# Moving the third set of transpositions and the projection behind half of the value products in a two-layer gated attention kernel

## The reference

```python
x = x + jnp.tanh(g_xattn[1]) * _L1_xattn_ref(_layernorm(x), ctx_1024, Wq, bq, Wk, bk, Wv, bv, Wo, bo)
# 16 heads of 8 features
q = (query_states @ Wq.T + bq)   # k and v likewise, from the context
scores = jnp.einsum('bhqd,bhkd->bhqk', q * SCALE, k)
attn = jax.nn.softmax(scores, axis=-1)
ctx = jnp.einsum('bhqk,bhkd->bhqd', attn, v)
out = ctx @ Wo.T + bo
```

## Time and profile before

| what | us |
|---|---|
| median of 3 runs | 304.81 (303.15 to 305.63) |
| the profiled execution, its own time | 303.55 |
| its span in the trace | 301.7 |
| PE busy | 277.1 (92%) |
| DVE busy | 236.2 (78%) |
| ACT busy | 130.8 (43%) |
| POOL busy | 85.5 (28%) |

### The profile page before, as it was taken

How to read it: one execution, slowest core, us unless ns; L and a number is a source line. 1 busy time by engine, 2 the same in 40 slices (tenths; PEclk the granted TensorE clock), 3 DMA queues, 4 the chain that set the end, 5 groups by cost and what they waited for, 6 DMA issues and landing times.

```text
span 301.7 us, 5454 instructions
## 1 busy us (share of the span) xinstructions
PE 277.1 (92%) x1646; PEld 208.5 (69%) x1646; DVE 236.2 (78%) x661; ACT 130.8 (43%) x275; POOL 85.5 (28%) x161
## 2 busy tenths in 40 slices
PE   6799899999989979869899899899999999999993
PEld 5588577667566557458788788798966676676661
DVE  4887889859988987887888888887578779776572
ACT  1497552342242242385565565565432332423320
POOL 7467010100480304322843943842100100000000
PEclk9999899999999999999999999999999999999999
DMA  6910059173262152000000000000242331521640
GB/s 212 352 53 1 4 172 245 54 235 106 55 187 76 61 174 75 0 2 0 2 1 2 2 0 3 0 2 1 80 133 70 118 131 35 185 95 33 209 147 35
DMA packets 15066, 25.26 MB, mean 84 GB/s; under 512 B 2341, under 2 KB 4339, under 8 KB 14835
## 3 DMA queue, kind: packets, MB, share of 16 engines
q1 hardware_dynamic: 12968, 23.88, 24.5%
q10 hardware_dynamic: 2072, 1.07, 1.3%
HBM read 22.98 MB, written 1.25 MB: 80 GB/s over the span
## 4 chain that ended last, share of the span: by engine, by line
PE 70%; DVE 8%; DMA 6%; ACT 5%; POOL 4%; issue 4%; SPq 0%; POOLq 0%; DVEq 0%; ACTq 0%
PE S L543 25%; PE Ybank L565 15%; PE Ybank L714 10%; DMA CR<-comb_rows 4%; PE bank L700 4%; PE S L690 3%; ACT pt L977 2%; DMA comb_rows<-ct 2%; PE Tb L483 2%; POOL KT L355 1%; PE bank L581 1%; DVE xn L1060 1%; PE Tb L728 1%; POOL xn L405 1%; DVE cmx L1337 1%
## 5 line engine op out<-in xcount | busy, mean ns | idle before, releaser
L862 ACT ACTIVATE sg<-S 128x512 f32<-128x512 f32 x64 | 38.0, 596 | 70.5 <-PE S L543 65.6
L1206 DVE TENSOR_TENSOR hb<-sg,CR 128x512 f32<-128x512 f32 x64 | 45.1, 705 | 13.9 <-DMA CR<-comb_rows 5.1
L1199 DVE TENSOR_TENSOR sg<-sg,S 128x512 f32<-128x512 f32 x64 | 43.5, 680 | 3.5 <-PE S L543 2.1
L338 POOL TENSOR_TENSOR rstd<-ve,mhalf 128x4 f32<-128x4 f32 x11 | 11.1, 1011 | 107.1 <-DVE ve L1053 107.1
L714 PE MATMUL Ybank<-VX,pt 128*128 128x128 f32 (+1 forms) x320 | 39.8, 275 | 0.0
L714 PEld LDWEIGHTS Ybank<-VX,pt 128*128 128x128 f32 (+1 forms) x320 | 37.9, 192 | 0.4
L543 PE MATMUL S<-xh,WBH 128*128 128x512 f32 x64 | 33.8, 529 | 3.1 <-DVE sg L1199 3.0
L543 PE MATMUL S<-xh,UPH 128*128 128x512 f32 x64 | 36.1, 564 | 0.0
L565 PE MATMUL Ybank<-hb,downw 128*128 128x512 f32 x64 | 33.0, 599 | 0.7 <-DVE hb L1206 0.7
L565 PE MATMUL Ybank<-hb,W2T 128*128 128x512 f32 x64 | 32.9, 597 | 0.0
L1337 DVE TENSOR_REDUCE cmx<-S 128x8 f32<-128x616 f32 x32 | 25.4, 794 | 4.6 <-PE S L690 4.3
(11 more groups left out here) (164 smaller groups left out, 500.6 us busy)
## 6 DMA issues: line engine op xcount, KB each, us to landing
CR<-comb_rows SPq DMA_DIRECT2D x64, 128.0 KB, 3.1
CR<-comb_rows SPq DMA_DIRECT2D x32, 256.0 KB, 3.3
w13raw<-in_w SPq DMA_DIRECT2D x1, 1088.0 KB, 10.9
X<-in_x SPq DMA_DIRECT2D x4, 256.0 KB, 6.3
upraw<-in_up SPq DMA_DIRECT2D x4, 256.0 KB, 4.3
out_x<-X SPq DMA_DIRECT2D x4, 256.0 KB, 3.3
cT<-in_ctxT SPq DMA_DIRECT2D x2, 308.0 KB, 5.6
CN<-in_ctx SPq DMA_DIRECT2D x1, 616.0 KB
```

What stands on the lines that cost most here:

```text
L862: A(sg[:, k % 2, :], Gb[k % 2][:], ACT.Silu).then_inc(m.s_done, 1)
L1199: V.tensor_tensor(sg[:, k % 2, :], sg[:, k % 2, :], Ub[k % 2][:], ALU.mult).then_inc(m.t2, 1)
L1206: V.tensor_tensor(hb[:, k % 2, :], sg[:, k % 2, :], CR[:, k % RING, :], ALU.mult).then_inc(m.h_done, 1)
```

## The change

In TensorE's pass, the first half of `c_mix` (block n-1) moves ahead of `c_project` and the third set of transpositions moves behind `c_project`. The new order is scores, first set, turn, second set, first half of the value products, projection, third set, wait for `c_fin` where there is one, `norm_T` or `c_query`, second half. In ScalarE's pass the copy of the third set moves behind the first half of the exponentials of block n+1. In VectorE's pass the maxima of the second half move ahead of the final addition. No instruction is added or removed.

```diff
--- before.py
+++ after.py
@@ -743,11 +743,11 @@
                     if n >= 2:
                         c_turn(*divmod(n - 2, GB))
                     c_transpose(g, t, 1)
-                    c_transpose(g, t, 2)
+                    if n:
+                        c_mix(*divmod(n - 1, GB), n == 1, 0)
                     if n >= 2:
                         c_project(*divmod(n - 2, GB))
-                    if n:
-                        c_mix(*divmod(n - 1, GB), n == 1, 0)
+                    c_transpose(g, t, 2)
                     if n >= 2 and (t < 2 or last and t == GB - 1):
                         pe.wait_ge(c_fin, START + n - 1)
                     if t == 0:
@@ -991,9 +991,9 @@
                     if t == GB - 1 and last:
                         m_route_tanh(mD, 0)
                     c_copy(g, t, 1, n == 0)
-                    c_copy(g, t, 2, n == 0)
                     if n + 1 < NB:
                         c_exps(*divmod(n + 1, GB), 0)
+                    c_copy(g, t, 2, n == 0)
                     if t == 0:
                         norm_hi(2 * NG + 2 + g, xh[:, slot(g + 1):slot(g + 1) + GT])
                     if t == 1 and not last:
@@ -1381,10 +1381,11 @@
                         route_top(mD, 0)
                         route_pick(mD, 0)
                         route_weights(mD, 0)
+                    if ahead:
+                        c_max(*divmod(n + 1, GB), 1)
                     if n >= 2:
                         c_final(*divmod(n - 2, GB))
                     if ahead:
-                        c_max(*divmod(n + 1, GB), 1)
                         c_center(*divmod(n + 1, GB), 1)
                     if t == 0:
                         norm_lo(2 * NG + 2 + g, g + 1)
```

## The result

| | before | changed |
|---|---|---|
| median of 16 runs each, us | 303.58 | 302.16 |
| ratio, 95% interval | | 0.9934 (0.9915 to 0.9954) |
| profiled execution, us | 303.55 | 302.13 |
| first score product of block 0's pass to first gate product of mixture D, us | 85.04 | 83.11 |

What follows compares the result with a forecast made beforehand. TensorE was taken to set the pace, busy 20.3 of 22.0 us. The terms 1.68 + 0.42 - 0.21 + 0.21 - 0.26 = 1.84 us, taken from 304.81, gave 303.0 us; range 301.0 to 304.8.

Steps and rivals of the forecast that it cites:

- The stall's price: TensorE's third set waits for ScalarE's copy of the first set in 11 blocks; 0.42 us per stalled block.
- The bracket's 0.23: The wait for the copy shown in block 6's TensorE rows, 0.23 us, taken as the stall's lower bound.
- VectorE just keeps up at t = 2: Blocks 2, 6, 10, 14: VectorE's subtraction allows the next scores at 4.58 against TensorE's 4.59; gain 0.42 us each.
- rival of a late VectorE: Addition or subtraction 0.4 us late at t = 2, so blocks 2, 6, 10 gain nothing; 304.2 us, chance 15%.
- The wait that takes the stall's place: Blocks at t = 0 and 1: TensorE waits for the final addition until 3.71 us; only 0.21 us gained in all.
- rival of the full gain: The wait for the final addition is hidden, so all 11 stalled blocks gain; 4.4 us, 300.4 us, chance 10%.
- t = 3: Blocks 3, 7, 11 end on the chain variances, power, keys and get 0.07 us longer each, -0.21 us.
- Last pass: Block 15 never stalled but waits for the final addition ahead of the routing transpose; it loses 0.26 us.
- ScalarE: Exponentials ahead of the third copy end by 4.0 us, before the next copy at 4.3; the reordering is hidden.
- The slower rival: The final addition, behind late second maxima in seven blocks, costs more than the stall; 3.8 us slower, 308.6, chance 5%.
- The time: Whole kernel: median 304.81 us less the summed gain of 1.84 us gives 303.0 us, 0.6% faster.

Runs made afterwards that it cites:

- e1: Changed kernel with VectorE's old order, the final addition ahead of the second maxima again; ratio 1.0028 to the kernel before, stage 86.52 us.
- e5: Changed kernel with the projection inside the first half of the value products and the final addition ahead of the second maxima at t = 0 and 1; 0.9812 of before.
- e4: Changed kernel with TensorE's new order only in blocks 1, 2, 6, 10 and 14; ratio 0.9921 to the kernel before, stage 82.96 us.
- e3: Changed kernel with TensorE's old order, keeping VectorE's and ScalarE's new ones; ratio 0.9971 to the kernel before, stage 84.32 us.
- e2: Changed kernel with ScalarE's old order, the third set's copy ahead of the exponentials' first half again; ratio 0.9918 to the kernel before.
- e8: Changed kernel with GpSimd's keys of block 4g+5 expanded at t = 2, behind the power and ahead of the normalisation; ratio 0.9869 to the kernel before.
- e6: Changed kernel with GpSimd's keys of block 4g+5 expanded at t = 2, ahead of the power and the normalisation; ratio 0.9997 to the kernel before.
- e7: Changed kernel with the edits of e5 and e6 together; ratio 0.9767 to the kernel before, stage 77.60 us.
- e9: Changed kernel with the edits of e5 and e8 together; ratio 0.9764 to the kernel before, stage 77.62 us.

## Why the forecast held, point by point

**The stall's price.** Right. 0.42 us by the spacing of starts, and blocks 2, 6, 10 and 14 lost 0.43. The bracket's 0.23 would have given about half. Block 1 was mis-sized: I took 0.42 there too, and it lost 0.57. Its rows in the kernel before:

```profile
134.55 0.60 PE L700 MATMUL Ybank<-CB,PX 128*104 128x128 f32 x4
135.50 0.41 PE L700 MATMUL bank<-CB,PX 128*128 128x128 f32 x2 [0.34 <-ACT pt L977]
```

The third set follows the second after 0.95 us, 0.51 more than the unstalled 0.44. No turn stands between the first and the second set there, so TensorE came to the wait 0.11 us sooner; block 1's own spacing would have given most of the difference.

**VectorE just keeps up at t = 2.** Right, and shown by undoing it (e1). The margin was 0.08 us before, and the swap of maxima and addition is a condition of the change, not an ornament: without it the stage is longer than before. The rival of a late VectorE falls for the changed kernel, and is exactly what e1 is. In e5 the subtraction of block 6 ends 0.44 us ahead of the next scores and the block still takes 4.58, so in the changed kernel's 4.57 it is TensorE's own work that sets the length.

**The wait that takes the stall's place.** Right in place and size. Forecast: `norm_T` and the query at 3.71; measured 3.70 and 3.69. e4 shows that these passes are worth 0.1 us at most, e5 that nothing else held them back by that much. The rival of the full gain falls for this change. In the changed kernel's trace the second half stands behind the waiting instruction in all seven places (in block 8 at 175.61, `norm_T` at 175.12). This agrees with the rule of the Trainium skill that the prediction cites ("TensorE: Matmul & The Clock Gate", Part 3), by which products start in program order.

**t = 3.** The size was right (+0.07), and so was the end of the chain, the keys. But I asked only how much later the power would start, not how much earlier VectorE's swap by itself would let it; e3 shows 0.23 us there. The change gives this up again: its projection is later, and with it VectorE's addition and subtraction.

**Last pass.** Right: +0.26.

**ScalarE.** Right for blocks 2 to 13, which in e2 move by at most 0.02 us, and for the pair 14 and 15, whose sum stays. Blocks 0 and 1 can't be read in e2, since the clock was low there.

**The slower rival** did not come: the addition started 0.03 us behind the projection in block 8 (174.74 to 174.77), and the second maxima had ended at 174.66. In the seven blocks that wait for it, the addition never stood behind late maxima.

**The time.** The forecast of 303.0 us stands on a median of 304.81 from 3 runs; the median of 16 is 303.58. The sum was right in place and size, and the 0.84 us by which the measured 302.16 lies below 303.0 come from that base. That -0.66% fits -0.6% so well is partly luck, since single runs of one kernel differ by 2.4 to 3.1 us.

What stays open: why the attention starts up to 3 us later in some profiles, and why the clock fell in blocks 0 and 1 of three profiles (e2, e5, e8) and in block 11 of e6. Neither was tried.

## What to carry to other kernels

Price a stall by the spacing of starts beside the same pair of instructions without the stall; the bracket shows only part of it (here 0.23 of 0.42, 0.17 of 0.33 and 0.34 of 0.57 us). Before work is moved out from between two instructions, ask what else it covered: here the value products hid both the copy and the final addition, and only an order that keeps cover for both (the projection split into the half) brings the whole gain. Where an engine has little slack, work out the engines that must follow in the same sum, and undo their part alone to see what it is worth.

## What the runs showed of the hardware

A VectorE instruction on 128x4 elements lasted 1.19 us in place of 0.17 when GpSimd had started a 1.21 us instruction 0.05 us before; the row shows no wait, only a long duration (e6). With GpSimd's five short copies beside it the same instruction took 0.24 us in e3 and 0.17 in e5, e7 and e9. So a move on GpSimd that looks free of dependencies has to be held against VectorE's rows at that time, and an order that makes it wait for the VectorE result can be worth more than an earlier start.

The granted clock fell to means of 0.55, 0.59 and 0.67 over 3.5 us behind a pause in which TensorE was busy 1.4 to 1.5 of 3.0 us, in three profiles (e2, e8, e5); the same pause was followed by 1.00 in the kernel before. e6 has both within one profile: the held-up turn left TensorE busy for 1.50 to 1.51 of 3.0 us in blocks 3, 7 and 11, and the clock stayed at 1.00 over the 3 us behind it in the first two and was 0.61 in the third, whose block became 1.6 us longer. In e5, e8 and e2 blocks 0 and 1 together were 0.1, 0.3 and 0.6 us longer, as much as the effects that were looked for, which is why the comparisons here go by single blocks.
